# Expert stage of a transformer layer on one Trainium2 core: a third place for incoming weights, and three pieces of work issued earlier

## The chip, the core and the metric

The kernel runs on one core of a Trainium2 chip, in one launch. The metric is the device time in microseconds (us) of the whole launch. The core has TensorE (PE, matrix products), VectorE (DVE), ScalarE (ACT), GpSimd (POOL) and SyncE (SP, which here only issues transfers), each with its own instruction queue, and 16 DMA engines between HBM and the on-chip memory. Engines wait for one another through semaphores.

## The reference

The input `x` has 512 rows of 512 numbers. Three stages are added to it one after the other: a cross attention over 8192 context rows, a state space block with a gated MLP, and a mixture of experts. Only the last stage is touched by the change. With `x` the layer-normed rows, it computes

```python
logits = x @ router_w.T                      # 16 experts
top_vals, top_idx = top_k(logits, 2)
gates = sigmoid(top_vals)
gate, up = split(x @ gate_up_w[e])           # per expert e: 512 -> 2 * 512
out_all[e] = (silu(gate) * up) @ down_w[e]   # 512 -> 512
moe = sum over the two chosen experts of gates * out_all
shared = (silu(x @ shared_gate_w.T) * (x @ shared_up_w.T)) @ shared_down_w.T   # width 1024
out = x_before_norm + moe + shared
```

## The kernel before

Everything ahead of the expert stage (some 2326 us) stays as it is. The expert stage is the function `experts`. It works on 25 sets of weights, `w` = 0 to 24. A set is 2 MB of gate and up weights and 1 MB of down weights, as 32-bit numbers. Sets 0 and 24 are the two halves of the shared expert. Sets 1 to 16 are the 16 experts, and sets 17 to 23 are seven extra turns for experts that got more than 128 rows; their expert number is computed by the kernel and read from a register (`value_load`).

Each product is made of three 16-bit products, so each set has to be split into a high and a low part. ACT writes the high parts (`gh`, `dh`, L1717 and L1710), DVE the low parts (`gl`, `dl`, L1811 and L1804). Incoming 32-bit weights land in places: two for gates (`gf`) and two for downs (`df`); set `w` uses place `w % 2`, and its load waits until the set that had the place is split.

The order of work is written out by hand in each engine's queue:

- PE transposes the rows, makes the router's logits (`lp`), and goes through `shared(0)`: for each of four column blocks `j` a gate product (12 matmuls) and an up product (12). After the first pair, `positions()` sums the choice masks into `pos` and `count`, which lie in the accumulator `op`. From them DVE works out in `places()` where each row goes, and in the end `expert`.
- POOL then scatters the rows to HBM (`xs_dram`) with eight indirect transfers (L1694), sorted into slots of 128 rows.
- There are 23 slots, `s` = 0 to 22, and slot `s` uses set `s + 1`. For PE a slot is: gate product (`project(s, 0)`), transposes of the slot before (`turn(s - 1)`), up product (`project(s, 1)`), transposes of the next slot's rows (`rows(s + 1)`, L2015), and the down products of the slot before (`down_slot(s - 1)`). In slot 0 the 48 matmuls of `down_shared(0)` stand between the two products. ACT copies the result to `yc` (L1758), and SP stores it.
- In slot `s` ACT and DVE split set `s + 2`. DVE in slot 0: low parts of two gate chunks, the product `smf`, four additions `add(0)` (L1823) that read what `down_shared(0)` left in `op`, then the low parts of the other two chunks and of the downs.
- SP's queue: loads of sets 1, 2 and 3, then the rows of slots 0 and 1 (once the scatter has landed), and then for each `s`: the store of slot `s - 1` (L1655), the rows of slot `s + 2` (L1651), and set `s + 4` (gates L1639, downs L1643).
- `shared(1)` and `down_shared(1)` close the stage. In the first column block PE also does `turn(22)` and `down_slot(22)`. ACT stores the last result to `yc` one column block later. POOL gathers the rows back into `yg` (L1701) once all stores have landed, DVE adds them with their weights (L1944, eight instructions), and then adds the shared result (L1823, four).

The loads before:

```python
def load(w):
    if w >= 2:
        sp.wait_ge(gl_ready, (w - 1) * DC)
    ...
    if w >= 2:
        sp.wait_ge(dl_ready, (w - 1) * 2)
```

Of the kernel before, what the change touches and what calls it, by code (L numbers as in the profile page):

```python
# [1547 lines left out]
TOP = 2  # L1548
# [4 lines left out]
def experts(nc, keep, xs_dram, ys_dram, wsplit, gate_up, down, out):  # L1553


    with ExitStack() as ctx:
        m = Space(nc, ctx, "ex")
        ex = ExpertPlaces(keep)
        gf, df = ex.gf, ex.df
        gh, gl = ([first, m.sb(n, [P, DC, 2 * EH], F16)] for n, first in (("gh", ex.gh[0]), ("gl", ex.gl[0])))  # L1560
        dh, dl = ([m.sb(f"{n}{i}", [P, EHC, D], F16) for i in range(2)] for n in ("dh", "dl"))
        sg, mf = m.sb("sg", [P, EHC, T]), m.sb("mf", [P, EHC, T])
# [19 lines left out]
        smh, sml = (m.sb(n, [P, EHC, P], F16) for n in ("smh", "sml"))  # L1582
        yc = [m.sb(f"yc{i}", [P, D]) for i in range(2)]
        yg = m.sb("yg", [P, TT, TOP, D])
        gp, up = m.ps("gp", [P, 2, T]), m.ps("up", [P, 2, T])
        op = m.ps("op", [P, TT, D])
        lp = up[:, 1, 0:TT * NE].rearrange("p (t e) -> p t e", e=NE)
# [2 lines left out]
        sgp, sup, smt = gp[:, 0, :], up[:, 0, :], up[:, 1, :].rearrange("p (j c) -> p j c", c=P)  # L1590
        sxt = gp[:, 1, :].bitcast(F16).rearrange("p (c n) -> p c n", n=P)

        g_in, d_in, x_in = ([m.sem(f"{n}{i}") for i in range(2)] for n in ("g_in", "d_in", "x_in"))
        w_in, made, consts = m.sem("w_in"), m.sem("made"), m.sem("consts")
        hT_ready, hh_ready, hl_ready, l_ready = (m.sem(n) for n in ("hT_ready", "hh_ready", "hl_ready", "l_ready"))
        lg_ready, sig_ready, ah_ready, al_ready = (m.sem(n) for n in ("lg_ready", "sig_ready", "ah_ready", "al_ready"))
# [17 lines left out]
        def own_slot(e):  # L1614
            return slice(e * P, (e + 1) * P)

        @block.sync
        def _(sp):
            at = DIC * 64
            for s, r in enumerate((rh, rl)):  # L1620
                sp.dma_start(r.rearrange("p c n -> p (c n)"), wsplit[s][:, W.SMALL[0], at:at + DC * NE]).then_inc(w_in, 16)
            gates_of = gate_up.rearrange("(e c p) n -> p e c n", p=P, c=DC)
            downs_of = down.rearrange("(e c p) n -> p e c n", p=P, c=EHC)

            def which(w):
                if w == SETS - 1:
                    return NE + 1
                if w <= NE:
                    return w - 1
                return sp.value_load(expert[0:1, w - 1 - NE:w - NE], min_val=0, max_val=NE - 1)  # L1630

            def load(w):
                par = w % 2
                if w >= 2:
                    sp.wait_ge(gl_ready, (w - 1) * DC)
                if w == 1 + NE:
                    sp.wait_ge(expert_ready, 1)
                e = which(w)
                sp.dma_start(gf[par], gates_of[:, bass.ds(e, 1), :, :].rearrange("p o c n -> p (o c) n")  # L1639
                             ).then_inc(g_in[par], 16)  # L1640
                if w >= 2:
                    sp.wait_ge(dl_ready, (w - 1) * 2)
                sp.dma_start(df[par], downs_of[:, bass.ds(e, 1), :, :].rearrange("p o c n -> p (o c) n")  # L1643
                             ).then_inc(d_in[par], 16)

            def load_rows(s):
                if s == 0:
                    sp.wait_ge(sent, 16 * TOP * TT)
                if s >= 2:
                    sp.wait_ge(sx_ready, s - 1)  # L1650
                sp.dma_start(xr[s % 2][:, :], xs_dram[own_slot(s), :]).then_inc(x_in[s % 2], 16)  # L1651

            def store(s):
                sp.wait_ge(yc_ready, s + 1)
                sp.dma_start(ys_dram[own_slot(s), :], yc[s % 2][:, :]).then_inc(y_out[s % 2], 16)  # L1655

            for w in range(1, 4):
                load(w)
            load_rows(0)
            load_rows(1)  # L1660
            for s in range(SLOTS):
                if s:
                    store(s - 1)
                if s + 2 < SLOTS:
                    load_rows(s + 2)
                if s + 4 < SETS:
                    load(s + 4)
            store(SLOTS - 1)
            for t in range(TT):
                sp.wait_ge(o_read, TT + TT + TOP * TT + t + 1)  # L1670
                sp.dma_start(out[t * P:(t + 1) * P, :], keep.x1[:, t, :]).then_inc(out_done, 16)
            sp.wait_ge(out_done, 16 * TT)

        @block.gpsimd
        def _(pool):
# [14 lines left out]
            for t in range(TT):  # L1690
                for k, place in enumerate((place1, place2)):
                    if t == 0:
                        pool.wait_ge(place_ready, k + 1)
                    nc.gpsimd.indirect_dma_start(  # L1694
                        out=xs_dram, out_offset=bass.IndirectOffsetOnAxis(ap=place[:, t:t + 1], axis=0),
                        in_=ah[:, t, :, :].rearrange("p s d -> p (s d)"), in_offset=None).then_inc(sent, 16)
            for par in range(2):
                pool.wait_ge(y_out[par], 16 * ((SLOTS + 1 - par) // 2))
            for t in range(TT):
# [6 lines left out]
        def _(act):  # L1706
            def split_down(w, p):

                cs = slice(2 * p, 2 * p + 2)
                nc.scalar.activation(dh[w % 2][:, cs, :], df[w % 2][:, cs, :], ACT.Copy, scale=SW).then_inc(dh_ready, 1)  # L1710

            def split_gates(w, cs):
                par = w % 2
                if cs[0] == 0:
                    act.wait_ge(g_in[par], 16 * ((w + 1) // 2 if par else w // 2))
                for c in cs:
                    nc.scalar.activation(gh[par][:, c, :], gf[par][:, c, :], ACT.Copy, scale=SW).then_inc(gh_ready, 1)  # L1717

            def down_in(w):
                act.wait_ge(d_in[w % 2], 16 * ((w + 1) // 2 if w % 2 else w // 2))  # L1720

            def high(h, j):
                act.wait_ge(mf_ready, h * EHC + j + 1 + 2)
# [2 lines left out]
            def shared(h):  # L1726


                for j in range(EHC):
                    act.wait_ge(g_ready, h * EHC + j + 1)  # L1730
                    nc.scalar.activation(sg[:, j, :], gp[:, j % 2, :], ACT.Silu, scale=UNSCALE).then_inc(sg_ready, 1)
                    if h and j == 0:
                        high_slot(SLOTS - 1)
                    if h and j == 1:
                        result(SLOTS - 1)
                    if j:
                        high(h, j - 1)
                    if h == 0 and j < 2:
                        split_gates(1, (2 * j, 2 * j + 1))
                    if h == 0 and j >= 2:  # L1740
                        if j == 2:
                            down_in(1)
                        split_down(1, j - 2)
# [49 lines left out]
        def _(dve):  # L1793
# [6 lines left out]
            def split_down(w, p):  # L1800

                cs, par = slice(2 * p, 2 * p + 2), w % 2
                dve.wait_ge(dh_ready, w * 2 + p + 1)
                nc.vector.scalar_tensor_tensor(dl[par][:, cs, :], df[par][:, cs, :], SW, dh[par][:, cs, :], ALU.mult,  # L1804
                                               ALU.subtract).then_inc(dl_ready, 1)

            def split_gates(w, cs):
                par = w % 2
                for c in cs:
                    dve.wait_ge(gh_ready, (w - 1) * DC + c + 1)  # L1810
                    nc.vector.scalar_tensor_tensor(gl[par][:, c, :], gf[par][:, c, :], SW, gh[par][:, c, :],  # L1811
                                                   ALU.mult, ALU.subtract).then_inc(gl_ready, 1)

            def low(h, j):
# [42 lines left out]
            def places():  # L1857
# [25 lines left out]
                own.done(nc.vector.reduce_sum(whose[:, :], done[:, :, :], AX.X))  # L1883
                nc.vector.tensor_scalar(expert[:, :], whose[:, :], float(NE - 1), None, ALU.min).then_inc(expert_ready, 1)

            def shared(h):
                for j in range(EHC):
                    dve.wait_ge(u_ready, h * EHC + j + 1)
                    dve.wait_ge(sg_ready, h * EHC + j + 1 + 2)
                    if h:  # L1890
# [3 lines left out]
                    if h == 0 and j == 0:  # L1894
                        weights()
                        places()
                    if h and j == 0:
                        low_slot(SLOTS - 1)
                    if j:
                        low(h, j - 1)  # L1900
                    if h == 0 and j < 2:
                        split_gates(1, (2 * j, 2 * j + 1))
                    if h == 0 and j >= 2:
# [33 lines left out]
            for s in range(SLOTS):  # L1937
                slot(s)
            shared(1)
            for t in range(TT):  # L1940
                dve.wait_ge(fetched[t], 16 * TOP)
                for k, g in enumerate((g1, g2)):
                    dve.wait_ge(o_read, TT + TT + TOP * t + k)
                    nc.vector.scalar_tensor_tensor(keep.x1[:, t, :], yg[:, t, k, :], g[:, t:t + 1], keep.x1[:, t, :],  # L1944
                                                   ALU.mult, ALU.add).then_inc(o_read, 1)
            add(1)

        @block.tensor
        def _(pe):
# [27 lines left out]
            def shared(h):  # L1977
                w = h * (SETS - 1)
                pe.wait_ge(gl_ready, w * DC + DC)
                for j in range(EHC):  # L1980
                    for half, bank, free, ready in ((0, gp, sg_ready, g_ready), (1, up, mf_ready, u_ready)):
# [15 lines left out]
                                ).then_inc(ready, 1)  # L1997
                        if h and j == 0 and half == 0:
                            turn(SLOTS - 1)
                    if h == 0 and j == 0:  # L2000
                        pe.wait_ge(lg_ready, 1)
                        positions()
                    if h and j == 0:
                        down_slot(SLOTS - 1)

# [45 lines left out]
            def slot(s):  # L2051
# [1 line left out]
                if s:  # L2053
                    pe.wait_ge(ssg_ready, s)
                project(s, 0, sgp).then_inc(sg_done, 1)
                if s == 0:
                    down_shared(0)
                else:
                    turn(s - 1)
                if s:  # L2060
                    pe.wait_ge(smf_ready, s)
                else:
                    pe.wait_ge(mf_ready, EHC + 2)
# [10 lines left out]
            for t in range(TT):  # L2074
# [2 lines left out]
                                          three(keep.hh[:, c, tok], keep.hl[:, c, tok], rh[:, c, :], rl[:, c, :])]  # L2077
                        ).then_inc(l_ready, 1)
            shared(0)
            rows(0)  # L2080
            for s in range(SLOTS):
                slot(s)
# [109 lines left out]
```

## Time and profile before

| | |
|---|---|
| median of 3 runs | 2650.38 us (2645.7 to 2653.98) |
| profiled execution, its own time | 2642.64 us |
| profiled execution, span from first to last instruction | 2640.9 us |
| mean granted TensorE clock | 0.964 of full speed |
| PE busy | 2408.8 us (91% of the span) |
| DVE busy | 1979.1 us (75%) |
| ACT busy | 1597.5 us (60%) |
| DMA queue issued by SP | 360.96 MB, 42.9% of 16 engines |
| expert stage | from about 2326 us to the end |

Busy shares are means over the whole span. The expert stage takes the last 315 us of it and has stretches of its own: the routing, a pause until the scattered rows are back, the 23 slots, and the second shared half.

### The profile page before, as it was taken

The numbers are of one execution on the slowest core, as the hardware profiler recorded it, in microseconds if no ns is written. First come the engines' busy times: TensorE is split into PE (matmuls) and PEld (weight loads), VectorE is DVE, ScalarE is ACT, GpSimd is POOL, SyncE is SP. The second block draws the span as 40 slices with busy tenths as digits, with TensorE's granted clock in tenths as the row PEclk, the third lists the DMA queues.
The fourth block names the chain that finished last, engine by engine and source line by source line (L and its number), as shares of the span: only waits on it lengthen the run. The fifth ranks groups of instructions, "written<-read, shape, count | busy, mean of one in ns | idle before, by whom it ended". The sixth has DMA issues, their size and how long they took to land. (4 is left out here: it accounts for less than half of the span.)

```text
span 2640.9 us, 39746 instructions
## 1 busy us (share of the span) xinstructions
PE 2408.8 (91%) x14143; PEld 1015.9 (38%) x14143; DVE 1979.1 (75%) x1961; ACT 1597.5 (60%) x1963; POOL 683.5 (26%) x475
## 2 busy tenths in 40 slices
PE   6999999999999599999999999995767778969998
PEld 2333333333333244444444444442322234434443
DVE  5777777777777688888888888885759982257885
ACT  5556555555554477777777777773354432137884
POOL 1555555555554200000000000000049970020001
PEclk9999999999999799999999999997879898979999
DMA  6245644644632873333333333324040005157994
GB/s 239 80 151 172 186 143 158 206 145 143 202 116 80 209 209 90 97 99 93 102 93 94 103 92 99 103 53 148 26 161 0 0 0 191 48 188 275 384 392 171
DMA packets 170930, 365.99 MB, mean 139 GB/s; under 512 B 12465, under 2 KB 83249, under 8 KB 167153
## 3 DMA queue, kind: packets, MB, share of 16 engines
q1 hardware_dynamic: 169586, 360.96, 42.9%
q0 software_dynamic: 1280, 4.20, 0.5%
q8 instruction: 38, 0.62, 0.1%
q14 instruction: 26, 0.21, 0.0%
HBM read 254.24 MB, written 106.68 MB: 137 GB/s over the span
## 5 line engine op out<-in xcount | busy, mean ns | idle before, releaser
L447 DVE TENSOR_REDUCE kv_mx<-kv_s 128x1024 f32 (+1 forms) x512 | 595.7, 1218 | 227.0 <-PE kv_s L477 227.0
L697 DVE TENSOR_TENSOR at_pl<-at_pf,at_ph 128x1024 f16<-128x1024 f32 x512 | 614.5, 1223 | 131.4 <-ACT at_ph L665 122.5
L671 ACT ACTIVATE at_pf<-at_st 128x1024 f32<-128x1024 f32 x512 | 497.2, 1028 | 194.1 <-PE at_st L756 194.1
L755 PE MATMUL at_st<-at_qh,at_k_cur 128*128 (+1 forms) x1024 | 390.5, 381 | 18.6 <-DMA at_ql<-m_dram 17.4
L756 PE MATMUL at_st<-at_ql,at_k_one 128*128 (+1 forms) x1024 | 389.0, 380 | 0.0
L665 ACT ACTIVATE at_ph<-at_pf 128x1024 f16<-128x1024 f32 x256 | 273.8, 1069 | 0.0
L720 PE MATMUL at_acc<-at_ph,at_vs 128*128 128x512 f16 x1024 | 242.4, 379 | 2.1 <-DVE at_pl L697 1.9
L75 POOL MEMSET pa_ident<- 128x128 f32 x1 | 0.2, 210 | 915.0 <-POOLq L60 915.0
L367 POOL TENSOR_TENSOR kv_ksl<-kv_kf,kv_ksh 128x512 f16<-128x512 f32 x128 | 148.0, 1156 | 247.2 <-ACT kv_ksh L395 247.2
L840 PE MATMUL kv_kp<-first_ch,first_wkh 128*128 128x512 f16 x512 | 195.1, 381 | 8.8 <-DVEq L438 8.8
L840 PE MATMUL kv_kp<-first_ch,first_wkl 128*128 128x512 f16 x512 | 194.9, 381 | 0.0
L840 PE MATMUL kv_kp<-first_cl,first_wkh 128*128 128x512 f16 x512 | 194.6, 380 | 0.0
L840 PE MATMUL kv_vp<-first_wvl,first_ch 128*128 128x512 f16 x512 | 194.6, 380 | 0.0
L840 PE MATMUL kv_vp<-first_wvh,first_ch 128*128 128x512 f16 x512 | 194.5, 380 | 0.0
L840 PE MATMUL kv_vp<-first_wvh,first_cl 128*128 128x512 f16 x512 | 194.2, 379 | 0.0
L392 ACT ACTIVATE kv_kf<-kv_kp,first_bks 128x512 f32<-128x512 f32 x128 | 87.4, 683 | 172.2 <-PE kv_kp L840 172.2
L399 ACT ACTIVATE kv_vf<-kv_vp 128x512 f32<-128x512 f32 x128 | 76.1, 594 | 184.2 <-PE kv_vp L840 184.2
L1340 PE MATMUL ms_yp<-ms_hc,ms_ident 128*128 128x512 f32 x256 | 135.7, 677 | 51.5 <-POOL ms_hc L1226 43.0
L371 POOL TENSOR_TENSOR kv_vs<-kv_vf,kv_vs 128x512 f16<-128x512 f32 x128 | 148.1, 1157 | 129.3 <-ACT kv_vs L401 129.3
L693 DVE CAST at_ph<-at_pf 128x1024 f16<-128x1024 f32 x256 | 176.1, 688 | 0.0
L755 PEld LDWEIGHTS at_st<-at_qh,at_k_cur 128*128 128x128 f16 x1024 | 100.2, 98 | 179.9 <-issue 54.6
L1242 POOL TENSOR_TENSOR ms_b<-ms_u,keep_big 128x1024 f32<-128x1024 f32 x64 | 149.2, 2353 | 0.6
(341 smaller groups left out, 3892.0 us busy)
## 6 DMA issues: line engine op xcount, KB each, us to landing
keep_big<-gate_up SPq DMA_DIRECT2D x25, 2048.0 KB, 9.3
vd<-kv_vs SPq DMA_DIRECT2D x16, 2048.0 KB, 7.7
at_k_cur<-kd SPq DMA_DIRECT2D x128, 256.0 KB, 3.8
at_vs<-vd SPq DMA_DIRECT2D x64, 512.0 KB, 3.9
keep_big<-down SPq DMA_DIRECT2D x25, 1024.0 KB, 10.0
kv_tf<-wpack SPq DMA_DIRECT2D x21, 1024.0 KB, 6.3
first_cf<-ctxT SPq DMA_DIRECT2D x16, 1024.0 KB, 13.4
kd<-kv_ksh SPq DMA_DIRECT2D x32, 512.0 KB, 9.8
```

The lines of the kernel that those rows point to most:

```text
L367: nc.gpsimd.tensor_tensor(ksl[par][:, n, :], kf[:, n % 4, :], ksh[par][:, n, :], ALU.subtract).then_inc(kl_ready, 1)
L371: nc.gpsimd.tensor_tensor(vs[par][:, hs, kt, DH:2 * DH], vf[:, n % 4, :].rearrange("p (h d) -> p h d", d=DH), vs[par][:, hs, kt, 0:DH], AL ...
L447: nc.vector.reduce_max(mx[:, bass.ds(g * (NH * TT) + 2 * (m - TT), 2)], s1[:, m % 3, :, :], AX.X).then_inc(s1_max, 1)
L665: nc.scalar.activation(ph[:, s % RING, :, :], pf[:, s % RING, :, :], ACT.Copy).then_inc(ph_ready, 1)
L671: nc.scalar.activation(pf[:, s % RING, :, :], st[:, s % HP % NST, :, :], ACT.Exp, scale=SCORE).then_inc(pf_ready, 1)
L693: nc.vector.tensor_copy(ph[:, s % RING, :, :], pf[:, s % RING, :, :]).then_inc(ph_own, 1)
L697: nc.vector.tensor_tensor(pl[:, s % RING, :, :], pf[:, s % RING, :, :], ph[:, s % RING, :, :], ALU.subtract).then_inc(pl_ready, 1)
L720: nc.tensor.matmul(acc[:, 0, :], vs[:, 2 * s + e, :], ph[:, s % RING, e, :], start=(s == 0 and e == 0), stop=False)
L755: nc.tensor.matmul(st[:, w % NST, e, :], k_cur[:, tile], qh[:, q], start=True, stop=False)
L756: last = nc.tensor.matmul(st[:, w % NST, e, :], k_one[:, tile], ql[:, q], start=False, stop=True)
L840: last = nc.tensor.matmul(out, a, b, start=(start and n == 0), stop=(stop and n == len(pairs) - 1))
L1242: nc.gpsimd.tensor_tensor(b[i % RB][:, :, :], u[:, :].unsqueeze(1).to_broadcast([P, HN, T]), bb[q], ALU.mult).then_inc(b_ready, 1)
```

## The change

It does five things, all in the expert stage:

1. Gates and downs get a third place each: the third gate place is the memory of `yg`, the third down place is that of `ah`, the rows that POOL scatters. Set `w` uses place `w % 3`, and a load waits for the set three before it. POOL's gather into `yg` gets a wait for the last gates to be split.
2. SP's queue is put in another order. Ahead of the slots: gates 1, downs 1, gates 2, gates 3, downs 3, gates 4, rows 0, rows 1, downs 2, downs 4. In the loop set `s + 5` is loaded in place of `s + 4`. The expert number is read from the register once for the gates and once more for the downs.
3. `down_shared(0)` stands directly behind `shared(0)`, ahead of `rows(0)`, with a wait for `expert_ready`.
4. `positions()` stands between the first gate product and the first up product of `shared(0)`.
5. In `shared(1)`, DVE makes the low part of slot 22 before it waits for the first up product. ACT makes the last result in the first column block. DVE adds the gathered rows of blocks 0 and 1 in the third column block, and those of 2 and 3 at the end.

```diff
+        gf = ex.gf + [yg.rearrange("p t k d -> p (t k d)").rearrange("p (c n) -> p c n", c=DC)]
+        df = ex.df + [ah.rearrange("p t s d -> p (t s d)").bitcast(F32).rearrange("p (c n) -> p c n", c=EHC)]
...
+        def arrivals(w):
+            return w // 3 + (w % 3 > 0)
...
-            def load(w):
-                par = w % 2
-                if w >= 2:
-                    sp.wait_ge(gl_ready, (w - 1) * DC)
+            def load_gates_up(w):
+                if w >= 3:
+                    sp.wait_ge(gl_ready, (w - 2) * DC)
                 if w == 1 + NE:
                     sp.wait_ge(expert_ready, 1)
                 e = which(w)
...
+            def load_down(w):
+                if w >= 3:
+                    sp.wait_ge(dl_ready, (w - 2) * 2)
+                e = which(w)
...
-            for w in range(1, 4):
-                load(w)
+            load_gates_up(1)
+            load_down(1)
+            load_gates_up(2)
+            load_gates_up(3)
+            load_down(3)
+            load_gates_up(4)
             load_rows(0)
             load_rows(1)
+            load_down(2)
+            load_down(4)
             for s in range(SLOTS):
                 if s:
                     store(s - 1)
                 if s + 2 < SLOTS:
                     load_rows(s + 2)
-                if s + 4 < SETS:
-                    load(s + 4)
+                if s + 5 < SETS:
+                    load_gates_up(s + 5)
+                    load_down(s + 5)
...
+            pool.wait_ge(gl_ready, SETS * DC)
             for par in range(2):
                 pool.wait_ge(y_out[par], 16 * ((SLOTS + 1 - par) // 2))
...
                     if h and j == 0:
                         high_slot(SLOTS - 1)
-                    if h and j == 1:
                         result(SLOTS - 1)
...
+            def chosen_rows(ts):
+                for t in ts:
+                    dve.wait_ge(fetched[t], 16 * TOP)
+                    for k, g in enumerate((g1, g2)):
+                        dve.wait_ge(o_read, TT + TT + TOP * t + k)
+                        nc.vector.scalar_tensor_tensor(keep.x1[:, t, :], yg[:, t, k, :], g[:, t:t + 1],
+                                                       keep.x1[:, t, :], ALU.mult, ALU.add).then_inc(o_read, 1)
+
             def shared(h):
                 for j in range(EHC):
+                    if h and j == 0:
+                        low_slot(SLOTS - 1)
                     dve.wait_ge(u_ready, h * EHC + j + 1)
...
-                    if h and j == 0:
-                        low_slot(SLOTS - 1)
                     if j:
                         low(h, j - 1)
+                    if h and j == 2:
+                        chosen_rows((0, 1))
...
             shared(1)
-            for t in range(TT):
...
+            chosen_rows((2, 3))
             add(1)
...
                         if h and j == 0 and half == 0:
                             turn(SLOTS - 1)
+                        if h == 0 and j == 0 and half == 0:
+                            positions()
                     if h == 0 and j == 0:
                         pe.wait_ge(lg_ready, 1)
-                        positions()
...
                 project(s, 0, sgp).then_inc(sg_done, 1)
-                if s == 0:
-                    down_shared(0)
-                else:
+                if s:
                     turn(s - 1)
-                if s:
                     pe.wait_ge(smf_ready, s)
...
             shared(0)
+            pe.wait_ge(expert_ready, 1)
+            down_shared(0)
             rows(0)
```

## Rows read from the trace of the kernel before

**Rows 1.** Stretches: length, busy PE, PEld, DVE, ACT, POOL, clock, DMA share, GB/s.
```profile
2356.00:2369.00 13.00, 0.06 (x1) 0.00 (x0) 3.06 (x5) 0.63 (x1) 4.32 (x4) 0.65 0.98 363
2369.00:2396.00 27.00, 22.53 (x99) 9.86 (x100) 8.31 (x10) 8.32 (x9) 0.00 (x0) 0.85 0.04 12
2396.00:2591.00 195.00, 183.48 (x1002) 90.79 (x1001) 171.58 (x168) 171.83 (x208) 0.00 (x0) 1.00 1.02 389
```
**Rows 2.** Chain that ended last, from the scatter into slot 1: start, length, what.
```profile
2360.27 6.17 DMA xs_dram<-ex_ah,ex_place
2366.46 2.55 DMA ex_xr<-xs_dram
2369.05 1.05 PE ex_gp L2015 x8
2370.12 1.03 ACT ex_xt L1748
2371.20 5.30 PE ex_gp L840 x12
2376.50 10.61 PE ex_op L840 x48
2387.11 2.60 PE ex_up L840 x12
...
2390.35 0.69 DVE keep_x L1823
...
2393.42 2.28 DVE keep_big L1811 x2
```
**Rows 3.** Timeline of PE, DVE and ACT around the pause.
```profile
2353.31 2.75 PE L840 MATMUL ex_up<-keep_hidden,keep_big 128*128 128x512 f16 x12
...
2358.44 0.68 DVE L1816 TENSOR_TENSOR ex_ml<-ex_mf,ex_mh 128x512 f16<-128x512 f32 x1
...
2377.03 3.88 ACT L1717 ACTIVATE keep_big<-keep_big 128x1024 f16<-128x1024 f32 x4
```
**Rows 4.** Timeline of SP's queue: gates 3, gates 4, stores of slots 0 and 19.
```profile
2353.72 0.37 SPq L1639 DMA_DIRECT2D keep_big<-gate_up  x1
...
2395.71 0.40 SPq L1639 DMA_DIRECT2D keep_big<-gate_up  x1
...
2403.29 0.34 SPq L1655 DMA_DIRECT2D ys_dram<-ex_yc  x1
...
2581.58 0.34 SPq L1655 DMA_DIRECT2D ys_dram<-ex_yc  x1
```
**Rows 5.** DMA issues, 2396 to 2590 us: count, KB each, median us to landing.
```profile
keep_big<-gate_up SPq DMA_DIRECT2D x21, 2048.0 KB, 9.3
keep_big<-down SPq DMA_DIRECT2D x21, 1024.0 KB, 10.2
...
ex_xr<-xs_dram SPq DMA_DIRECT2D x20, 256.0 KB, 5.1
```
**Rows 6.** Waits, 2396 to 2590 us: us in total, times, longest.
```profile
PE ex_gp L2015 <- DMA ex_xr<-xs_dram: 11.2, 17, 1.4
```
**Rows 7.** Timeline of PE, ACT, POOL and DVE at the end.
```profile
2607.71 0.38 PE L840 MATMUL ex_op<-ex_dh,ex_smh 128*128 128x512 f16 x1 [1.43 <-issue]
...
2636.39 0.38 PE L840 MATMUL ex_op<-ex_dh,ex_ml 128*128 128x512 f16 x1
...
2613.58 0.59 ACT L1758 ACTIVATE ex_yc<-ex_op 128x512 f32<-128x512 f32 x1
...
2616.45 1.38 POOL L1701 DMA_INDIRECT ex_yg<-ys_dram,ex_place  x1 [255.21 <-DMA ys_dram<-ex_yc]
...
2625.79 0.95 POOL L1701 DMA_INDIRECT ex_yg<-ys_dram,ex_place  x1 [0.30 <-issue]
...
2628.03 6.46 DVE L1944 SCALAR_TENSOR_TENSOR keep_x<-ex_yg,ex_g,keep_x 128x512 f32<-128x512 f32 x8
2634.61 3.08 DVE L1823 SCALAR_TENSOR_TENSOR keep_x<-ex_op,keep_x 128x512 f32<-128x512 f32 x4
```

More of the change, by code:

```diff
@@ L1558, in experts @@
         ex = ExpertPlaces(keep)
-        gf, df = ex.gf, ex.df
         gh, gl = ([first, m.sb(n, [P, DC, 2 * EH], F16)] for n, first in (("gh", ex.gh[0]), ("gl", ex.gl[0])))
@@ L1591, in experts @@
         sxt = gp[:, 1, :].bitcast(F16).rearrange("p (c n) -> p c n", n=P)
-        g_in, d_in, x_in = ([m.sem(f"{n}{i}") for i in range(2)] for n in ("g_in", "d_in", "x_in"))
+        g_in, d_in = ([m.sem(f"{n}{i}") for i in range(3)] for n in ("g_in", "d_in"))
+        x_in = [m.sem(f"x_in{i}") for i in range(2)]
         w_in, made, consts = m.sem("w_in"), m.sem("made"), m.sem("consts")
@@ L1638, in load @@
                 e = which(w)
[L1639 to L1644, printed above, removed]
+                sp.dma_start(gf[w % 3], gates_of[:, bass.ds(e, 1), :, :].rearrange("p o c n -> p (o c) n")
+                             ).then_inc(g_in[w % 3], 16)
+            def load_down(w):
+                if w >= 3:
+                    sp.wait_ge(dl_ready, (w - 2) * 2)
+                e = which(w)
+                sp.dma_start(df[w % 3], downs_of[:, bass.ds(e, 1), :, :].rearrange("p o c n -> p (o c) n")
+                             ).then_inc(d_in[w % 3], 16)
             def load_rows(s):
@@ L1709, in split_down @@
                 cs = slice(2 * p, 2 * p + 2)
-                nc.scalar.activation(dh[w % 2][:, cs, :], df[w % 2][:, cs, :], ACT.Copy, scale=SW).then_inc(dh_ready, 1)
+                nc.scalar.activation(dh[w % 2][:, cs, :], df[w % 3][:, cs, :], ACT.Copy, scale=SW).then_inc(dh_ready, 1)
             def split_gates(w, cs):
@@ L1714, in split_gates @@
                 if cs[0] == 0:
-                    act.wait_ge(g_in[par], 16 * ((w + 1) // 2 if par else w // 2))
+                    act.wait_ge(g_in[w % 3], 16 * arrivals(w))
                 for c in cs:
-                    nc.scalar.activation(gh[par][:, c, :], gf[par][:, c, :], ACT.Copy, scale=SW).then_inc(gh_ready, 1)
+                    nc.scalar.activation(gh[par][:, c, :], gf[w % 3][:, c, :], ACT.Copy, scale=SW).then_inc(gh_ready, 1)
             def down_in(w):
-                act.wait_ge(d_in[w % 2], 16 * ((w + 1) // 2 if w % 2 else w // 2))
+                act.wait_ge(d_in[w % 3], 16 * arrivals(w))
             def high(h, j):
@@ L1803, in split_down @@
                 dve.wait_ge(dh_ready, w * 2 + p + 1)
-                nc.vector.scalar_tensor_tensor(dl[par][:, cs, :], df[par][:, cs, :], SW, dh[par][:, cs, :], ALU.mult,
+                nc.vector.scalar_tensor_tensor(dl[par][:, cs, :], df[w % 3][:, cs, :], SW, dh[par][:, cs, :], ALU.mult,
                                                ALU.subtract).then_inc(dl_ready, 1)
@@ L1810, in split_gates @@
                     dve.wait_ge(gh_ready, (w - 1) * DC + c + 1)
-                    nc.vector.scalar_tensor_tensor(gl[par][:, c, :], gf[par][:, c, :], SW, gh[par][:, c, :],
+                    nc.vector.scalar_tensor_tensor(gl[par][:, c, :], gf[w % 3][:, c, :], SW, gh[par][:, c, :],
                                                    ALU.mult, ALU.subtract).then_inc(gl_ready, 1)
@@ L1939, in _ @@
             shared(1)
-            for t in range(TT):
[L1941 to L1945, printed above, removed]
+            chosen_rows((2, 3))
             add(1)
```

## The prediction

> **What bounds the kernel now.** The change touches only the expert stage, so I first cut that stage into stretches by the busy time of the engines [rows 1]. From 2356 to 2369 us PE does nothing while the DMA engines are 98% busy: it waits for scattered rows. From 2369 to 2396 the DMA engines are 4% busy and PE works, but part of the time at half speed (granted clock 0.85 in the mean). From 2396 to 2591, the slots, the DMA engines are 102% busy at 389 GB/s, and PE is busy 183.5 of 195 us.
>
> Then the chain of waits says what sets the start of the slots [rows 2]. The last scatter lands at 2366.44, the rows of slot 0 take 2.55 us more, and PE begins at 2369.05. Its eight transposes take 1.05 us and the gate product 5.30, against 2.60 for the up product of the same size later: these are the 1.2 and 2.4 GHz levels of the clock. Between the products stand the 48 matmuls of `down_shared(0)`, 10.61 us. Then DVE adds and splits, and the gates of set 2 are split at 2395.70. SP sends gates 4 at 2395.71 [rows 4], and from there the DMA engines never rest.
>
> In the slots one period is (2581.58 - 2403.29) / 19 = 9.38 us between stores [rows 4]. Each period moves a set, one slot of rows in and one of results out: 3.5 MB of 1024 KB, or 3.67 MB, which at 389 GB/s take 9.4 us. That is the period. What PE waits for in this stretch is not weights, however, but the small transfer of rows, 11.2 us in 17 waits [rows 6]. It takes 5.1 us in the median [rows 5], against 2.55 us on idle DMA engines [rows 2], because it stands in SP's queue behind the set issued one turn earlier. So the slots are bound by bytes per second, and the rows are where PE feels it.
>
> **The change, part by part.**
>
> *`down_shared(0)` ahead.* PE ends the last up product at about 2353.31 + 2.75 = 2356.1 [rows 3] and would now begin on the down products. The accumulator banks are free: the new wait for `expert_ready` is over by then, since DVE makes it at the end of `places()`, ahead of the scatter and of all `ml`. The last low part `ml` is there at 2358.44 + 0.68 = 2359.1 [rows 3]; 9 of the 48 matmuls come before it, 39 after. At 10.61 / 48 = 0.221 us each (this includes a few at the low clock) the end is 2359.1 + 8.6 = 2367.7. Behind the new wait stand only PE's own rows and slots, which could not have begun then.
>
> *When the rows of slot 0 arrive.* Until the scatter starts, SP now has gates 3 and downs 3 (3.15 MB) in the queue earlier; they no longer follow at 2353.7 and after. In their place gates 4 follow at about 2353.7, since it waits for the same split of set 1 as gates 3 did [rows 4]. Downs 4 and downs 2 come behind the rows. At 389 GB/s the 3.15 MB moved forward take 8.1 us, partly in time when the DMA engines had been idle, and 1.05 MB (downs 3 in the contended time) goes away: 2.7 us. The last scatter should land between 2363.7 (2.7 earlier) and 2368 (1.5 later, if the early loads hold up the first scatters), and the rows 2.55 us later, 2366.3 to 2370.6. I take the early end, as there is less traffic beside the last scatters. Then PE is the later one, at 2367.7.
>
> *Slot 0 anew.* PE goes from down products to transposes without a long pause and stays at 2.4 GHz: transposes 0.5 (half of 1.05), ACT's copy 1.03, gate product 2.60, with 0.07 between them: 2371.9. The up product follows at once and ends at 2374.5. ACT begins to split set 2 0.53 us after the gate product, as before (2377.03 against 2376.50), each chunk taking 0.97 [rows 3]. DVE's first two low parts end at about 2371.9 + 0.53 + 1.0 + 2.28 = 2375.7, so now they are ahead of `smf` on the path; before they lay under the down products. `smf` takes 0.64 (2390.35 less the end of the up product, 2389.71), to 2376.35. From the first addition to the end of the gates' split it took 2395.70 - 2390.35 = 5.35 us [rows 2], so the gates of set 2 are split at 2381.7 instead of 2395.7. **This saves 14.0 us.** In parts: 1.35 by the start, 0.55 and 2.70 by the clock, 10.61 by the down products, less about 1.3 for DVE's first parts that are no longer covered. If the rows come at 2370.6, it is 11.1.
>
> *The third place.* In the loop, load `s + 5` waits for the split of set `s + 2`; load `s + 4` waited for the same one. So each turn sends the same bytes at the same point, and the rows of the next turn again stand behind a full set. The weights come a slot earlier than needed, and nobody waited for them. Gates 4 and downs 4 move into the idle 27 us [rows 1], but gates 5 then begin where gates 4 began. All later events move with the start, and the periods stay 9.38. The store and row transfers are not delayed. **I take 0.** The bounds are a saving of 11.2 us, all of PE's waits for rows [rows 6], and on the other side 1.2 us, if each of the 20 periods is 0.06 longer. The second register read ahead of the downs (eight turns) delays only their issue; 10.2 us lie between issue and landing [rows 5], so other transfers cover it, and without this cover it would cost below 1 us in each of eight turns.
>
> *Mask sums ahead.* The fourteen small matmuls change place with an up product. DVE reads their result behind its own list (splits, low part of `ah`, `mf`), which ends later in either order: 0, and at most the length of these matmuls, some 0.4 us, in either direction.
>
> *The end.* PE waited 1.43 us for DVE's low part of slot 22 [rows 7]; now it is made while the up product runs: 1.43, and about 0.15 for the restart. From there PE runs through to its last matmul, which ended at 2636.77. DVE had eight additions of 0.81 us in a row before the last four, and began the very last at 2637.00, 0.23 behind PE [rows 7]. With four of them in a gap of the third column block, PE sets the end alone: 0.2 more. This needs the gathers: the last store no longer waits for the second gate product (L1758 ended at 2614.2, and could be 4.6 us earlier), so POOL's start moves from 2616.45 to about 2611.8 on the old clock, and the eight gathers follow one another by (2625.79 - 2616.45) / 7 = 1.33 us: the four for blocks 0 and 1 are issued by 2617. The additions that need them come after the third column block, about 2620 (PE's end less 10.4 for the last down products, 5.2 for one block and 1.5), which leaves some 3 us for landing. POOL's new wait for the last split (about 2600) lies under its wait for the stores. **This saves 1.7 us** (bounds 0 and 2.5).
>
> **The sum.** 14.0 + 0 + 1.7 = 15.7 us. Against the profiled execution: span 2640.9 to 2625.2, its own time 2642.64 to 2626.9. The median of the runs shown is 7.7 us above that execution, so from 2650.38 it is **2634.7 us**.
>
> **The rivals.**
>
> *A: the third place frees the slots.* With a set in hand PE could run at its own speed, if the rows were not held up. Then PE's waits of 11.2 us go too: 2634.7 - 11.2 = 2623.5. Against it: 102% DMA share over 195 us [rows 1] leaves no room for faster periods with the same bytes. Beside this stands a rule of the Trainium skill, "DMA: Bandwidth & Descriptors", section "Queues, rings and completion order": descriptors of one ring are consumed in order, but completion is not first in, first out per issuing engine. By its first half the rows stay behind the set and the sum stays; only if the second half let 256 KB overtake 3 MB by much would A hold, with the same 2623.5. The trace agrees with the first half, 5.1 us against 2.55. Chance 0.08.
>
> *B: part of the start is lost.* In the new slot 0 PE has two pauses, of about 2.4 us (for ACT's second copy, behind four splits) and 2.0 (for DVE), with two chunks of product between them. They are longer than PE's pauses at this point before. If the clock falls, slot 1 pays what slot 0 paid: 2.70 + 0.55. Together with rows at 2370.6 (2.9 later) and nothing gained at the end, 15.7 shrinks to 7.9: 2642.5. A fall already in the short pause at 2358 would give 10 us back (48 matmuls at double the length) and end at 2645. "TensorE: Matmul & The Clock Gate" of the Trainium skill (Part 1) says that the throttled state is the default and activity releases it; by it such thin stretches speak against the change, at B's price. The trace agrees in so far as PE came out of its 13 us pause at half speed. Chance 0.15.
>
> *C: slower.* The transfers in the slots get slower with three sets in flight over more memory. They carry 20 x 3.67 = 73.4 MB, 188.7 us at 389 GB/s. At 359 GB/s they would take 15.7 us more and eat the whole saving; below 346 GB/s the kernel is slower by over 0.3%, and at 335 it takes 2634.7 + 30.4 = 2665. For it speaks only that the rate is set outside the engines; against it that the pattern, the sizes and the order of transfers stay. Chance 0.03.
>
> *D: no effect.* The rows come so late that the down products hid nothing. It needs a scatter 8 us later than now. Since the same bytes pass with fewer idle stretches, I give it 0.02 at 2645 to 2652.
>
> **How the numbers follow.** The forecast has 0.72, with a range of its own of 2629 to 2640: 3 us of uncertain steps either way, and a median of a few runs that scatter by 4 us either way. The range must take in A and the milder part of B: 2621 to 2644. 0.3% is 8 us, and this is about what a measurement of this kernel can tell from no change. Faster by more: forecast, A and over a third of B, 0.87; within: most of B and D, 0.09; slower: C and the tail of D, 0.04.
>
> **What would show it.** In the profile after, the 48 down products should begin near 2356 and end near 2368, the gate product of slot 0 take 2.6 us, and gates 5 be issued at about 2382. Between the stores of slots 0 and 19 there should be 178 us as before, with 102% DMA share and again some 11 us of waits for rows; less than 170 would be A, more than 185 C. A granted clock under 1.00 between 2372 and 2390 would be B. At the end PE should have no pause ahead of `down_slot(22)`, and POOL start its gathers about 19 us earlier (14.0 + 4.6). I am wrong if the rows of slot 0 land after 2371, or if periods in the slots differ by more than 0.3 us.

## The result, and the profile after

| | before | after |
|---|---|---|
| median | 2651.9 us (5 runs) | 2635.21 us (5 runs, 2632.54 to 2637.61) |
| ratio | | 0.9944, 95% interval 0.993 to 0.9958 |
| profiled execution, its own time | 2642.64 us | 2637.61 us |
| its span | 2640.9 us | 2635.9 us |

The forecast was 2634.7 us and a saving of 15.7 us. The ratio gives 14.9 us (interval 11 to 19); the two medians differ by 16.7. The two profiled executions differ by only 5.0 us, and this has to be explained before the rows are compared.

First the chain of waits of the kernel after, from the scatter into slot 1, which answers to [rows 2] (start, length, what):

```profile
2364.72 5.08 DMA xs_dram<-ex_ah,ex_place
2369.81 2.86 DMA ex_xr<-xs_dram
2372.72 0.63 PE ex_gp L2037 x8
2373.38 1.03 ACT ex_xt L1764
2374.45 2.78 PE ex_gp L840 x12
...
2379.97 1.22 DVE keep_big L1827
2381.19 0.60 DVE ex_smf L1944
...
2384.77 2.28 DVE keep_big L1827 x2
```

SP's queue after, which answers to [rows 4] (router weights, with which the expert stage begins for SP; then gates 5; then the stores of slots 0 and 19):

```profile
2330.74 0.35 SPq L1628 DMA_DIRECT2D ex_rh<-wsplit  x1
...
2387.07 0.37 SPq L1645 DMA_DIRECT2D ex_yg<-gate_up  x1
...
2394.64 0.34 SPq L1664 DMA_DIRECT2D ys_dram<-ex_yc  x1
...
2578.06 0.34 SPq L1664 DMA_DIRECT2D ys_dram<-ex_yc  x1
```

In the profile before, the same router load was issued at 2326.26. So the expert stage began 4.5 us later in this execution, although nothing ahead of it was changed. That is scatter: over thirteen profiles of this document the issue lies between 2324.52 and 2330.74. All times of the stage have to be read from this issue. Counted so, the first gates of the slot loop are sent at 56.3 us instead of 69.4 (13.1 earlier; forecast 14.0), the store of slot 0 at 63.9 instead of 77.0, and from the store of slot 19 to the end of the span it takes 57.8 us instead of 59.3. Between these two stores, however, the kernel after took 183.4 us and the kernel before 178.3, or 9.65 and 9.38 us a period.

The end after, from the timelines of POOL and DVE and the chain, answers to [rows 7]:

```profile
2603.06 2.59 PE ex_op L840 x12
```
```profile
2609.11 0.98 POOL L1718 DMA_INDIRECT ex_yg<-ys_dram,ex_place  x1 [243.43 <-DMA ys_dram<-ex_yc]
...
2617.25 3.17 DVE L1907 SCALAR_TENSOR_TENSOR keep_x<-ex_yg,ex_g,keep_x 128x512 f32<-128x512 f32 x4
...
2631.99 0.69 DVE L1839 SCALAR_TENSOR_TENSOR keep_x<-ex_op,keep_x 128x512 f32<-128x512 f32 x1 [1.90 <-PE ex_op L840]
```

`down_slot(22)` follows the up product with no pause, half of the gathered rows are added in the third column block, and the last addition waits for PE alone.

What the end gained is best read from a point that the rows of the slots no longer touch, the first gate product of the second shared half. Before and after:

```profile
2600.49 2.76 PE L840 MATMUL ex_gp<-keep_hidden,keep_big 128*128 128x512 f16 x12 [1.77 <-DVE keep_big L1811]
```
```profile
2597.27 2.76 PE L840 MATMUL ex_gp<-keep_hidden,keep_big 128*128 128x512 f16 x12 [1.77 <-DVE keep_big L1827]
```

From there to the end of the span it took 40.4 us before and 38.6 after, 1.8 less.

Much of what made the slots longer shows in the timeline of PE, 2554 to 2559 us. It waited 2.16 us for rows, and then its matmuls went to half speed:

```profile
2554.28 0.62 PE L2037 MATMUL ex_gp<-ex_ident,ex_xr 128*128 128x128 f16 x8 [2.16 <-DMA ex_xr<-xs_dram]
...
2554.95 0.38 PE L840 MATMUL ex_op<-ex_dl,ex_smh 128*128 128x512 f16 x1
...
2557.08 0.63 PE L840 MATMUL ex_op<-ex_dl,ex_smh 128*128 128x512 f16 x1
```

This period took 12.67 us, 3.3 more than the mean before; the other 1.8 of the 5.1 us are spread over the stretch. The experiments had to tell whether that belongs to the change.

### The profile page after: what moved, and what is told of

Same layout as the page of the kernel before. It is cut to its first block and busy times, and to the rows that moved or that the text cites. A ratio compares the mean times of both kernels' runs of the same rounds, so it can differ in the third digit from the quotient of the medians.

```text
span 2635.9 us, 39768 instructions
## 1 busy us (share of the span) xinstructions
PE 2410.1 (91%) x14143; PEld 1015.8 (39%) x14143; DVE 1978.0 (75%) x1961; ACT 1597.8 (61%) x1963; POOL 683.7 (26%) x475
```

## The experiments

Counts in us "after the stage's start" are from the issue of the router weights, as above. Ratios are to the kernel before, run beside them, and savings are worked out from the ratios unless the text says medians.

**The changed kernel again** (no edit).

> The changed kernel once more, as the measure for the three beside it. Own theory (the order of PE's work gives the gain, the third place nothing): 15 us faster than before, ratio near 0.994, as in its first runs. The profile of its first run had 183.4 us between the stores of slots 0 and 19 against 178.3 before. If that is caused by the change (rival: the third place or the second register read makes the slots longer) this profile has over 181 again; if it is scatter from run to run, 176 to 181.

Median 2633.9 us, ratio 0.9938 (0.9922 to 0.9954). First loop gates at 56.2 us, store of slot 0 at 63.8, 187.1 us between the two stores with two periods above 12.6, 57.3 to the end. By the bound I had set this spoke for longer slots through the change; the second profile of the kernel before (below) then showed the same length there.

**Down products ahead, alone** on the kernel before:

```diff
                 project(s, 0, sgp).then_inc(sg_done, 1)
-                if s == 0:
-                    down_shared(0)
-                else:
+                if s:
                     turn(s - 1)
...
             shared(0)
+            pe.wait_ge(expert_ready, 1)
+            down_shared(0)
             rows(0)
```

> The kernel before with one part of the change: the down products of the first shared half ahead of slot 0. Own theory: the rows of slot 0 land as before, so 12.7 us (the 14.0 less 1.35 for the start) are saved, ratio 0.995; gates 4 are issued at about 2383 instead of 2396. Rival (the third place and the early loads carry the gain): at most 5 us, ratio over 0.998.

Median 2639.37 us, ratio 0.9963 (0.995 to 0.9976): 9.8 us. First loop gates at 57.8 us, 11.6 earlier. But the store of slot 0 came only 10.3 us earlier, since the clock fell in slot 1. Chain of waits of this kernel there:

```profile
2386.79 2.74 PE ex_gp L840 x6
2389.53 0.85 PE ex_up L2035 x4
2390.38 2.69 PE ex_up L840 x12
```

Six matmuls took 2.74 us, about what twelve took in slot 0 of the kernel after. Expected were 12.7 us from the start; this one edit carries two thirds of the whole gain.

**Two places with all else of the change.** Loads, places and waits as in the kernel before:

```diff
-        gf = ex.gf + [yg.rearrange("p t k d -> p (t k d)").rearrange("p (c n) -> p c n", c=DC)]
-        df = ex.df + [ah.rearrange("p t s d -> p (t s d)").bitcast(F32).rearrange("p (c n) -> p c n", c=EHC)]
+        gf, df = ex.gf, ex.df
...
+            for w in range(1, 4):
+                load(w)
             load_rows(0)
             load_rows(1)
```

> The changed kernel without the third place: two places and the loads in the order of before, all else as changed. Own theory: 12.7 us at the start and 1.7 at the end, 14.4 together, ratio 0.9946, within 2 us of the changed kernel. Rival (the third place carries the gain): 5 us or less, ratio over 0.998. If the third place costs time in the slots: 3 us or more better than the changed kernel.

Median 2641.02 us of seven executions, ratio 0.9953 (0.9936 to 0.997). The first of the seven, the profiled one, took 11,167 us, with PE 99% busy, and nothing is read from it; the median of the other six is 2639.7. The kernel ran again:

> Two places with all else of the change, once more for a usable profile. Own theory: gates 4 issued some 58 us after the stage's start, 12 to 14 us saved in all, ratio 0.995; the changed kernel lies within 2 us of it. Rival (the third place is worth something by itself): 4 us or more slower than the changed kernel.

Median 2640.35 us, ratio 0.996 (0.9946 to 0.9973). Together some 11.5 us, against 15 to 16 with the third place. First loop gates at 60.1 us, store of slot 0 at 69.5: the clock was low twice, in slot 0 and in slot 1. 183.0 us between the stores. So the third place and its loads are worth some 5 us: 4 to 5 by the ratios, 6 to 8 by the medians of the kernels with three places that ran beside these (2633.9 and 2632.76). I had expected at most 2, and 4 or more was the mark of the rival that the third place is worth something by itself. The profile puts it at the start (the store of slot 0 comes 5.6 us later than in the kernel after), not in the slots.

**Down products put back,** the third place kept:

```diff
                 project(s, 0, sgp).then_inc(sg_done, 1)
+                if s == 0:
+                    down_shared(0)
+                else:
+                    turn(s - 1)
                 if s:
-                    turn(s - 1)
                     pe.wait_ge(smf_ready, s)
...
             shared(0)
-            pe.wait_ge(expert_ready, 1)
-            down_shared(0)
             rows(0)
```

> The changed kernel with the down products put back between the two products of slot 0; the third place and all else stay. Own theory: some 1.7 us at the end and at most 2 at the start, ratio 0.998 to 1.000. Rival (third place carries the gain): 8 us or more, ratio under 0.997.

Median 2647.99 us, ratio 0.9992 (0.9983 to 1.0001), about 2 us. First loop gates at 68.9, 180.0 us between the stores, 57.6 to the end. The rival that the third place carries the gain is out.

**One register read per set:**

```diff
-                    load_gates_up(s + 5)
-                    load_down(s + 5)
+                    load_down(s + 5, load_gates_up(s + 5))
```

> The changed kernel with the expert number read from the register once per set, not again ahead of the downs. In both profiles of the changed kernel the periods of slots 12 to 18 were longer than in the kernel before. Own theory: the second read is covered and the long periods are scatter; same time as the changed kernel within 1.5 us. Rival (the second read delays the queue): 3 us or more better, and no period over 10.5 us after slot 12.

Median 2632.76 us, ratio 0.994 (0.9927 to 0.9954), as the changed kernel. 185.7 us between the stores. None of the periods after slot 12 was over 10.5 us, which I had given the rival as a mark, but a period of 12.70 stood between the stores of slots 9 and 10 and the time stayed. The second read costs nothing that can be measured.

**The kernel before again** (no edit).

> The kernel before once more, for a second profile. Its first profile was 7.7 us under the median, and had 178.3 us between the stores of slots 0 and 19; the changed kernel's had 183.4 and 187.1. If the first one was a lucky execution: 181 to 187 here, and no real difference in the slots. If the change makes the slots longer: 177 to 180.

2651.61 us, and 185.4 us between the stores, with a period of 12.79 in which the mean granted clock was 0.87. The first profile of before had the shortest stretch of all with two row buffers. Over the nine profiles with two row buffers the stretch took 178.3 to 188.1 us. The four with three places have a mean of 184.1 (183.4, 187.1, 185.7, 180.0), the five with two places 183.0 (178.3, 185.4, 188.1, 180.1, 183.0). The change does nothing to the slots that can be told from scatter. This is a weak zero: with single profiles 7 to 10 us apart in each group, the means leave room for a few us either way.

**The three edits of the end alone** on the kernel before (the hunks of `low_slot`, `result` and `chosen_rows` shown in the change):

> The kernel before with the three edits of the end alone (low part of slot 22, last result, half of the gathered rows earlier). Own theory: 1.7 us, ratio 0.9990 to 0.9996, and 57.6 us from the store of slot 19 to the end in place of 59.3. Rival (the edits of the end explain a good part of the gain): over 4 us.

Median 2646.66 us, ratio 0.9998 (0.9988 to 1.0008): too small for the timed runs. The profile has 57.8 us from the store of slot 19 to the end, against 59.3 and 60.4 in the two profiles before; but three slots lie in this stretch too, with their scatter. From the first gate product of the second shared half it takes 38.6 us here, as in all nine profiles of kernels with these three edits (38.60 to 38.66), and 40.4 in all four without them (40.40 to 40.45). So the edits of the end save 1.8 us.

**Four row buffers.** If PE feels the transfers only through the rows, they can be asked for a turn earlier. On the changed kernel:

```diff
+XR = 4
...
-        xr = [m.sb(f"xr{i}", [P, 2 * D], F16) for i in range(2)]
+        xr = [m.sb(f"xr{i}", [P, 2 * D], F16) for i in range(XR)]
...
-                if s >= 2:
-                    sp.wait_ge(sx_ready, s - 1)
...
+                if s >= XR:
+                    sp.wait_ge(sx_ready, s - XR + 1)
...
+            load_rows(2)
             for s in range(SLOTS):
...
-                if s + 2 < SLOTS:
-                    load_rows(s + 2)
+                if s + XR - 1 < SLOTS:
+                    load_rows(s + XR - 1)
```

> The changed kernel with four buffers for rows in place of two, so that the rows of a slot are asked for one turn earlier, ahead of the set that held them up. Own theory: PE's waits for rows go, PE runs at 8.66 us a slot on the weights that the third place holds ahead, until the last set's landing sets the end. First loop gates at 56 us after the stage's start, 73.4 MB at 385 GB/s are 191 us, so the last gates land near 246 and are now wanted near 241, where they were wanted near 257: 8 to 11 us better than the changed kernel, ratio to the kernel before 0.990. Rival (bytes per second alone set the slots, whoever waits): within 2 us of the changed kernel.

**Median 2612.98 us, ratio 0.9865 (0.985 to 0.988).** That is 35 us less than before and 20 less than the changed kernel, twice what I had expected. 164.4 us between the stores, all 19 periods at 8.65 or 8.66. The same with two places and all else of the change:

> Four row buffers, but only two places for weights and the old order of loads; all else of the change. Own theory: now PE waits for weights instead of rows, as each set lands only 1 to 2 us ahead of its split; within 3 us of the kernel with two places and two row buffers, and 5 us or more slower than the one with three places and four row buffers. Rival (rows ahead alone are enough): as fast as with three places.

Median 2623.48 us, ratio 0.9906 (0.9891 to 0.9921), 169.5 us between the stores. I had expected it within 3 us of the kernel with two places and two row buffers, and it was 17 us faster by the medians. And on the kernel before, nothing else changed:

> The kernel before with four row buffers and nothing else changed. With two places and the rest of the change this gave some 14 us. Theory now (the slots were bound by the loop of store, rows and PE, not by bytes per second): periods of 9.03 us, which is 3.67 MB at 406 GB/s, and 10 to 14 us less, ratio near 0.995. Rival (it needs the new start): under 5 us.

Median 2636.23 us, ratio 0.9952 (0.9936 to 0.9967), 172.3 us between the stores: 12.7 us less, as expected, and without the new start. These rows are of the stretch between the two stores, by busy time (columns as in [rows 1]). The kernel before, its second profile:

```profile
2404.05:2589.46 185.41, 169.05 (x913) 83.24 (x912) 155.58 (x153) 157.75 (x191) 0.00 (x0) 0.99 1.00 375
```

Kernel before with four row buffers:

```profile
2403.54:2575.79 172.25, 166.64 (x912) 82.63 (x911) 156.09 (x153) 157.40 (x191) 0.00 (x0) 1.00 1.04 403
```

Changed kernel with four row buffers:

```profile
2389.67:2554.08 164.41, 164.41 (x913) 83.16 (x912) 155.64 (x153) 157.00 (x191) 0.00 (x0) 1.00 1.04 405
```

In the last one PE is busy without a gap. The bytes of a turn are the same in all three, and the rate rises from 375 to 405 GB/s. Who set the length of the stretch shows in the chains of waits. One turn of the first profile before, from store to store:

```profile
2439.99 0.34 SPq L1655
...
2440.38 5.05 DMA ex_xr<-xs_dram
...
2445.48 0.62 PE ex_gp L2015 x8
2446.10 2.60 PE ex_op L840 x12
...
2448.72 0.61 ACT ex_yc L1758
...
2449.35 0.34 SPq L1655
```

The transfer of rows is 51.8% of the chain between the two stores there. In the kernel before with four row buffers transfers of gates have this place, with 52.8%. In the changed kernel with four row buffers the chain of this stretch is PE alone:

```profile
by line: PE ex_op L840 30.0%; PE ex_up L840 30.0%; PE ex_gp L840 29.9%; PE ex_gp L2039 5.2%; PE ex_up L2059 5.1%
```

What the rows of those three kernels took to land (DMA issues, same stretch and order):

```profile
ex_xr<-xs_dram SPq DMA_DIRECT2D x19, 256.0 KB, 5.3
```
```profile
ex_xr<-xs_dram SPq DMA_DIRECT2D x19, 256.0 KB, 7.1
```
```profile
ex_xr<-xs_dram SPq DMA_DIRECT2D x19, 256.0 KB, 9.0
```

They land later, but are asked for a turn earlier, so PE no longer waits for them. With two places somebody waits again, for weights. Waits in that stretch of the kernel with two places, four row buffers and all else of the change (us in total, times, longest):

```profile
ACT ex_gh L1725 <- DMA keep_big<-gate_up: 1.9, 7, 0.3
ACT keep_big L1725 <- DMA keep_big<-gate_up: 1.9, 7, 0.3
```

There is a bound by bytes per second after all, only a faster one. With two places and the rows ahead most periods are 9.00 to 9.06 us, and 3.67 MB in 9.03 us are 406 GB/s. The kernel with three places runs at 8.65 us, in which 405 GB/s bring only 3.50 MB. It lives on the set that it holds ahead: 66.5 MB were moved between the two stores, against 69.4 in the other two rows above, and the rows took 6.6 us to land in the first quarter of the stretch and 11.8 in the last. By this the slots would fall back to some 9.05 us if there were many more of them (an estimate from these numbers; no run has more slots).

**Additions later.** On top of three places and four row buffers, in slot 0:

```diff
-                if s == 0:
-                    add(0)
                 split_gates(w + 1, (2, 3))
+                if s == 0:
+                    add(0)
```

> Three places, four row buffers, and in slot 0 DVE's four additions behind the split of the last two gate chunks of set 2. Theory: gates 5 are sent 3 us earlier (53.4 us after the stage's start, from 56.4), PE's pause there becomes short, so the clock does not fall; slot 1 gives back some 1.6 us because the low part of slot 0 is then late. 1.4 to 3 us better than with the additions in their old place, ratio 0.9855. Rival: the low part of slot 0 eats all of it, within 1 us.

Median 2613.79 us, ratio 0.9871 (0.9855 to 0.9886): no gain. Gates 5 were sent at 54.1 us, 2.4 earlier, but the store of slot 0 came at 63.8, as ever. The gate product of slot 1 had no more pause within it and was slow instead:

```profile
2380.07 4.45 PE L840 MATMUL ex_gp<-keep_big,ex_xt 128*128 128x512 f16 x12 [2.35 <-ACT ex_xt L1766]
```

Both what I had expected (no fall of the clock) and the rival's reason (the low part of slot 0) were wrong. The pause of 2.35 us for ACT's copy stayed, and the slow product, 1.9 us longer than at full speed, took back most of the 2.4 us.

## Why the prediction was right, point by point

**Down products ahead: right.** They began at 2360.34 and ended at 2372.2 in the profile after, 29.6 to 41.5 us after the stage's start. Forecast were 29.8 and 41.4. Alone they save 9.8 us by the ratio.

**When the rows of slot 0 arrive: the early end was wrong.** I took 2366.3, or 40.0 us after the stage's start. They landed at 2372.67, at 41.9: only 0.8 earlier than before. The transposes then waited 0.5 us for them, so this cost 0.5. My mark for being wrong, rows after 2371, is 44.7 us on the clock of the stage, and was not passed. The last scatter was issued at 34.0 us in both kernels (2364.72 here, 2360.27 in [rows 2]) and took 5.08 us to land instead of 6.17: 1.1 earlier, where I had hoped for 2.7. The rows themselves took 2.86 us instead of 2.55.

**Slot 0 anew: right.** The gate product took 2.78 us instead of 5.30. Gates 5 came 13.1 us earlier (13.2 in the second profile) where 14.0 was the term; of the missing 0.9, the late rows account for 0.5.

**The third place: the size was right for the slots, the reason was not.** I took 0, and the slots show none that stands out from scatter. Over the whole it was worth some 5 us, through the start: with the down products ahead, the rows came up to 2 us earlier than with the loads in the old order (issued at 39.1 us against 40.5 and 41.2), and in neither profile of the changed kernel did the clock fall there. The first is a matter of the loads: in all six profiles with the new order the rows were issued at 39.1 to 39.5 us. The second is not shown to be: with one register read, three places and the same loads, the clock fell. With the down products in their old place none of it counts, since that kernel gained 2 us in all, 1.8 of them at the end.

The failed step is "the slots are bound by bytes per second". I took 389 GB/s and a DMA share of 1.02 for the limit. With four row buffers the same engines moved 405 GB/s at 1.04, and the period was 9.03 us on two places and 8.65 on three. The period of 9.38 was the round trip from the store through the rows behind a full set to PE's transposes and down products and back to the store (in the turn shown above, 5.05 of 9.36 us for the rows), and since SP sends the next set behind the store, this came later as well. The forecast of 0 came out all the same, because its other reason was right: nobody waited for weights. What I held against rival A, that a share of 102% leaves no room, was wrong: PE's waits for rows could go, and 20 us with them, but not by this change. In the slots the third place pays only once the rows are ahead. Between the kernels with two and three places there (2623.48 against 2612.98) lie 10.5 us, 5.1 of them between the stores of slots 0 and 19; another 5.3 are at the start, as without the rows ahead.

**Mask sums ahead: 0, not tried alone.** No run shows its share.

**The end: right in the profile.** 1.8 us from the first gate product of the second shared half (38.6 against 40.4, the same in every profile), where 1.7 was the term. POOL began its gathers 31.1 us after the store of slot 19 instead of 34.9, 3.8 earlier where 4.6 was forecast.

**The sum.** 13.1 + 0 + 1.8 = 14.9 us by the profiles, 14.9 by the ratio, 15.7 forecast. Only 5.0 of it is seen between the first two profiles, because there the stage began 4.5 us later, the slots between the two stores took 5.1 us longer, and the last ones 0.3. That the median came within 0.5 us of the forecast is in part luck: the term of the start was 0.9 too large, the ratio's interval is 7 us wide, and the median before, 2650.38 in the forecast, was 2651.9 over five executions.

**Rival B was underrated in how often it occurs.** With the down products ahead and the additions in their old place there are seven profiles, and its fall of the clock in slot 0 or 1 is in four of them: the down products alone, two places with two and with four row buffers, and one read. Read from the way between first loop gates and store of slot 0 (7.6 us without it; 8.9, 9.4, 9.4 and 9.2 with it, and on two places 1.7 more in slot 0), it cost 1.3 to 3.5 us. In the kernel with the down products alone it was 1.3, and the rows landed at 43.4 us instead of 42.7; the two explain most of why its store of slot 0 came 10.3 us earlier and not 12.7. Why it stayed away in the two profiles of the changed kernel and in the one with four row buffers is open: the first pause is 2.35 us in all seven. For **C** I had named 185 us between the stores as the mark. The second profile of the changed kernel passed it (187.1), but so did the kernel before (185.4), so the mark was badly chosen: C did not occur. The same holds for my mark of 0.3 us between periods. The kernel after had 0.27 more than the first profile before, its second profile 0.46, and the second profile of the unchanged kernel 0.38. Of the other marks for the slots, the DMA share was 1.01 where 1.02 was forecast, and PE's waits for rows were 14.1 us where some 11 were (10.5 and 16.1 in the two profiles before). Nor did D occur.

## What to carry to other kernels

A busy share near 100% of the DMA engines is no proof of a bound: ask which transfer somebody waits for, and try what happens when only that one is asked for earlier. More room for data that nobody waits for gives nothing in the loop until the small transfer queued behind it is ahead too. Here the 19 periods between the stores took 183.0 us in the mean with two places and two row buffers, 184.1 with three places, 170.9 with four row buffers, and 164.5 with both. Before two profiles are subtracted, check stretches that the change didn't touch, and take a second profile of the kernel before when the difference sought is below 1%. Measure an edit between two points that enclose it and nothing that scatters: the 1.8 us of the end could not be told in the timed runs, and agreed within 0.1 us in thirteen profiles.

## What the runs showed of the hardware

The rate of the 16 DMA engines on one mix of 256 KB to 2 MB transfers was higher when the rows were asked for a turn earlier: 370 to 391 GB/s between the stores when the rows landed in 4.8 to 5.6 us in the median (nine profiles), 400 to 405 when they landed in 7.1 to 9.8 (four). In the nine profiles with two row buffers PE paused ten times between these stores for 2.0 us or more, each time for rows. After six of these pauses (2.16 to 3.57 us) its matmuls fell from the 2.4 to the 1.2 GHz level, 0.38 to 0.63 us each, as in the period of 12.67 us above; after the other four (2.03 to 3.00 us, the longest with two places and all else of the change) they stayed at 0.38. The length of the pause alone did not decide it.
